# Second attention: turned rows, remote part, combination and local gate one round later, weight sum ahead of the last block transpose

## What is computed

```python
local = _local_window_attn(Q, K, V)
...
lp = jax.nn.softmax(lsc, axis=-1)
rem = jnp.einsum('bhsn,bhnd->bhsd', lp, GV)
rem = rem.transpose(0, 2, 1, 3).reshape(Bx, Sx, LATENT_DIM) @ r_out_w
...
gl = jax.nn.sigmoid(jnp.einsum('bhsd,hd->bhs', Q, gate_local_w))[..., None]
gr = jax.nn.sigmoid(jnp.einsum('bhsd,hd->bhs', Q, gate_remote_w))[..., None]
out = gl * local + gr * rem
out = out.transpose(0, 2, 1, 3).reshape(Bx, Sx, D_MODEL)
return out @ w_out
```

## Time and profile before

| | |
|---|---|
| median of 3 runs | 1703.9 us (1700.4 to 1706.74) |
| the profiled execution | 1714.27 us, its span 1712.6 us |
| busy: PE, DVE, ACT, POOL | 1511.4, 1137.9, 989.6, 931.1 us |
| mean granted clock of PE | 0.936 |

### The profile page before, as it was taken

One profiled execution on the slowest core, in us unless ns is written; L12 is line 12 of the kernel. 1 busy time (PEld: TensorE's weight loads), 2 busy tenths in 40 slices (PEclk: granted clock), 3 DMA queues, 4 the chain that ended last, 5 costly groups with the idle time before them and its releaser, 6 DMA issues.

```text
span 1712.6 us, 44507 instructions
## 1 busy us (share of the span) xinstructions
PE 1511.4 (88%) x13886; PEld 1087.7 (64%) x13887; DVE 1137.9 (66%) x2702; ACT 989.6 (58%) x2495; POOL 931.1 (54%) x1633
## 2 busy tenths in 40 slices
PE   7989999999999999998999688888888888885884
PEld 5645455555555555555999577777777777774774
DVE  5666555555555555552555498898898998995662
ACT  5544455555555555553334588888888888872442
POOL 5334555555555555554543466666666666631665
PEclk6989899999999999998999699999999999995776
DMA  9131132222211212223332122211211212215442
GB/s 278 34 83 42 51 82 57 57 57 57 55 49 52 55 50 54 55 57 73 67 68 62 30 48 45 45 41 43 46 43 41 45 43 42 44 38 113 86 93 35
DMA packets 240853, 103.39 MB, mean 60 GB/s; under 512 B 145497, under 2 KB 229274, under 8 KB 240794
## 3 DMA queue, kind: packets, MB, share of 16 engines
q1 hardware_dynamic: 230554, 89.04, 22.4%
q0 software_dynamic: 10240, 13.64, 3.8%
HBM read 57.73 MB, written 35.96 MB: 55 GB/s over the span
## 4 chain that ended last, share of the span: by engine, by line
PE 46%; ACT 16%; DVE 10%; DMA 10%; issue 7%; POOL 5%; SPq 5%; POOLq 0%; DVEq 0%; ACTq 0%
PE bankA L1887 5%; PE bankB L1933 5%; DMA remainders<-yT 4%; PE bankT L1916 4%; PE bankT L2067 4%; SPq L369 3%; DMA dq<-remainders 3%; DVE mneg L1000 3%; ACT qx L1692 3%; ACT km L1701 2%; ACT gqx L1692 2%; PE bankS L1901 2%; PE bankB L1937 2%; PE bankT L1919 2%; PE bankB L2130 2%
## 5 line engine op out<-in xcount | busy, mean ns | idle before, releaser
L682 POOL TENSOR_SCALAR_AFFINE_SELECT probs<-probs 128x512 f32<-128x512 f32 x256 | 184.0, 743 | 154.1 <-ACT probs L1578 154.1
L1578 ACT ACTIVATE probs<-bankT 128x1024 f32<-128x1024 f32 x128 | 131.1, 1024 | 190.6 <-PE bankT L1919 190.6
L999 DVE TENSOR_REDUCE mneg<-bankS 128x2 f32<-128x256 f32 x256 | 106.6, 417 | 160.2 <-PE bankS L1906 159.4
L1000 DVE TENSOR_REDUCE mneg<-bankS 128x2 f32<-128x512 f32 x256 | 174.3, 681 | 0.0
L675 POOL CAST qb<-qT 128x256 bf16<-128x256 f32 x256 | 97.5, 400 | 92.4 <-ACT qT L1573 91.7
L1916 PE MATMUL bankT<-qT,kT 37*128 37x512 f32 x512 | 138.0, 617 | 9.5 <-ACT probs L1580 6.2
L1573 ACT ACTIVATE qT<-bankA,bd 128x256 f32<-128x256 f32 x256 | 107.6, 473 | 65.5 <-PE bankA L1887 65.5
L1887 PE MATMUL bankA<-xnT,wd 128*128 128x256 f32 x480 | 144.4, 414 | 0.0
L1933 PE MATMUL bankB<-probs,vaug 128*64 128x512 f32 x512 | 142.9, 637 | 1.0 <-ACT yT L1585 1.0
L1585 ACT COPY yT<-bankB 128x512 f32<-128x512 f32 x128 | 75.1, 587 | 116.7 <-PE bankB L1937 116.7
L1367 DVE STREAM_TRANSPOSE pt<-pe 128x768 f32<-128x768 f32 x128 | 124.4, 972 | 25.9 <-ACT pe L1678 25.9
(11 more groups left out here) (320 smaller groups left out, 4286.8 us busy)
## 6 DMA issues: line engine op xcount, KB each, us to landing
rzb<-reciprocals SPq DMA_DIRECT2D x128, 128.0 KB
yT<-yT SPq DMA_DIRECT2D x64, 128.0 KB
xtab<-tab SPq DMA_DIRECT2D x32, 192.0 KB, 2.0
xs_sorted<-zeros SPq DMA_DIRECT2D x1, 4608.0 KB, 19.0
qT<-xs_sorted SPq DMA_DIRECT2D x144, 32.0 KB, 1.8
ys_sorted<-qT SPq DMA_DIRECT2D x36, 128.0 KB, 1.9
value_rows<-vrow SPq DMA_DIRECT2D x32, 128.0 KB, 1.8
vx<-value_rows SPq DMA_DIRECT2D x256, 16.0 KB, 1.8
```

The source lines that it names most:

```text
L682: pool.affine_select(out=blocks, in_=blocks, compare_op=ALU.is_ge, fill=0.0, base=0, pattern=[[0, 4], [1, P]], channel_multiplier=-1).then ...
L1000: dve.tensor_reduce(mneg[:, n.half, :, j, 1], bankS[:, :, 128:384], AX.X, ALU.max, negate=True).then_inc(S["red_done"], 1)
L1578: act.activation(pT[:, g % 2].rearrange("p e j t -> p e (j t)"), bankT[:, 0:2, :], ACT.Exp, scale=SCALE0).then_inc(S["exp_done"], 1)
```

## The change

POOL: `local_gate` of the batch before (`p`, a new argument) moves from the end of the round to behind `stream1` and `copy1`. DVE: `turn_rows` moves to the place of `combine`, `combine` goes behind the third group's `shift`, `finish` behind the second `turn`, and `weight_sum` ahead of the fourth `turn`. PE: `remote` takes the place of `project`, and `project` goes behind the value product, ahead of the gate product. What is left over for the last batch is issued behind the loops. No instruction of work is added or taken away. Later lines of the changed kernel have numbers one or two higher.

```diff
-            def step1(b, n, m, k):
+            def step1(b, p, n, m, k):
                 if m:
                     stream1(m)
                     copy1(m, True)
+                if p:
+                    local_gate(p)
                 if n:
                     weigh(n)
...
                 if m:
                     pool_latents(m)
-                if b:
-                    local_gate(b)
                 if k:
                     gather(k)
...
             with pool.Fori(1, LOOP - 1) as i:
-                step1(Batch(i, 0), Batch(i, 1), Batch(i + 1, 0), Batch(i + 1, 1))
-                step1(Batch(i, 1), Batch(i + 1, 0), Batch(i + 1, 1), Batch(i + 2, 0))
...
+                step1(Batch(i, 0), Batch(i, 0).before(), Batch(i, 1), Batch(i + 1, 0), Batch(i + 1, 1))
+                step1(Batch(i, 1), Batch(i, 0), Batch(i + 1, 0), Batch(i + 1, 1), Batch(i + 2, 0))
...
+            local_gate(Batch(LOOP, 1))
...
                 if b:
                     shift(b, 1)
                 if p:
-                    combine(p)
+                    turn_rows(p)
                 if b:
                     turn(b, 0)
                     shift(b, 2)
                 if p:
-                    finish(p)
+                    combine(p)
                 if b:
                     turn(b, 1)
+                if p:
+                    finish(p)
                 if n:
                     route(n)
...
                 if m:
                     mean1(m, True)
+                if n:
+                    weight_sum(n)
                 if b:
                     turn(b, 3)
-                if n:
-                    weight_sum(n)
-                if b:
                     shared_gated(b)
                     shared_hidden(b)
                     invert1(b)
                 if n:
                     shift(n, 0)
-                if b:
-                    turn_rows(b)
...
+            turn_rows(Batch(LOOP, 1))
             combine(Batch(LOOP, 1))
             finish(Batch(LOOP, 1))
...
                 if n:
                     latents(n, b is not None)
                 if p:
-                    project(p)
+                    remote(p)
                 if b:
                     scores(b, 3)
                 if n:
                     values(n)
+                if p:
+                    project(p)
                 if b:
                     gate(b)
                     attend(b, 0, n is None)
...
                     xt1(m, b is not None)
-                if b:
-                    remote(b)
...
+            remote(Batch(LOOP, 1))
             project(Batch(LOOP, 1))
```

## The result

The changed kernel takes 1848.7 us (median of 4 runs, 1844.9 to 1853.4) against 1702.8 for the kernel before, measured beside it: a ratio of 1.0856, 95% interval 1.0822 to 1.0889. The forecast was 1871, its range 1812 to 1930. The profiled execution took 1848.92 us, its span 1846.0, at a mean granted clock of 0.900. Lines of DVE, ACT and PE have numbers one higher than before; POOL's line 868 has kept its number.

A forecast was written before the change was run, and what follows sets the result against it. The second attention was taken as bound by a loop of waits. 29 x (4.29 stall + 1.5 clock) - 1.2 = 167 us on the profiled 1714.3 gave 1881, less 10.4 for the median: 1871 us, range 1812 to 1930.

The forecast's parts named there:

- The bound: Second attention stage, 985 to 1546 us: a loop of waits of 18.07 us a round, no engine filling it.
- The stall: DVE waits before aT for POOL's gate product, now behind the gather: 4.29 us more a round, in 29 rounds.
- The fallen clock: PE, idle 4.5 us a round, drops to half clock for 5 us once work returns: 1.5 us per round.
- the room that hides it: PE's attention products end 6.13 us after aT, DVE's last transpose 7.41; of these 1.28 us, 1.0 taken as hiding lateness.
- The sum of weights: On DVE, ahead of the last transpose: free during its 0.57 us wait for the last exponential, otherwise 0.30 us.
- The link taken out: Turned rows, remote part, then query product at the round's end: without it ACT's qs starts 0.42 us earlier per round.
- The rival "faster": Product done before DVE reaches aT, by 4.3 us after xp, so no stall: 31 x 0.42 = 13 us, 1691; chance 0.03.

The follow-up runs named there:

- The kernel with PE kept busy: The changed kernel with four unread 128x512 products added on PE ahead of the projection, filling its idle time: 1827.1 us, ratio 1.0732.
- three pairs: Weight sum ahead of, then behind the last transpose: product before gathered stream 1708.1, 1699.2; product at round's end 1696.6, 1688.6; product and turned rows back 1682.9, 1690.0 us.

## Why the prediction was right, and where it was off

*The bound.* Right: the stage is a loop of waits. That PE, DVE, ACT and POOL all do less per microsecond in the changed kernel says the same.

*The stall.* Right in place and count, and near in size. The product was to end 8.89 us after xp and aT at 9.31; in the round above they end at 1169.79 and 1170.31, 8.68 and 9.20 after the end of xp (1161.11). The stall was put at 4.29 us a round, 123 us in all. The kernel with PE kept busy, which has the stall without the fallen clock, is 124 us above the kernel before (117 by its turned rows). The wait itself is longer than the 4 us and more of the working, 5.0, as DVE came to aT 1164.89 - 1161.11 = 3.78 us after xp and not 4.3. That the product's place is the cause is shown from both sides: moved alone it costs 193 us, moved back alone the loss is gone.

*The fallen clock.* Right that it falls, and when; **its size is the step that failed**: 1.5 us a round was forecast, 0.75 to 0.86 measured. The half clock lasted a little longer with work at hand (from 1170.4 to past 1176, some 6 us) than the 5 us taken, and PE fell behind by about half of that, as the working had it: its third group of attention products ended at 1178.71 + 0.41 = 1179.12, 8.81 us after aT, where 6.13 was read at full clock, so 2.7 us late.

```profile
1178.71 0.41 PE L2192 MATMUL bankT<-gvx,pt 128*64 128x68 f32 x8
```

```profile
1181.85 0.26 ACT L1768 COPY rows<-bankT 32x128 f32<-32x128 f32 x1
```

What was mis-sized is the room that hides it, put at 1.0. From aT to the last transpose took 7.65 us (working: 7.41), and from there to the last rows 1182.11 - 1177.96 = 4.15 (3.34): 1.05 came out in this round and some 1.6 were hidden. The sum had found 1.28 and used 1.0 of it. It also missed that in the kernel before PE's third group already ended 0.37 us behind DVE's last transpose (1162.81 against 1162.44), so that this much lateness stands in the 3.34 already; with it the room is 1.65. The forecast's 1.5 less the measured 0.75, 29 times, is 22 us: what 1871 was too high by.

The Trainium skill (TensorE: Matmul & The Clock Gate, section on the clock gate) would have kept the clock within one per cent of the span. The runs show 21.6 us, 1.2% of 1848.7, give or take some 9: near that advice, and not the 44 of the forecast.

*The sum of weights.* Put at nothing while DVE waits, 0.30 where it doesn't. In the changed kernel it cost nothing, as the late PE covered it (the last two groups of products are 0.71 us apart at the median with the sum in either place). Where the stall was taken away, two of three pairs show 0.22 to 0.23 us a round; in the third PE came later than the transpose.

*The link taken out* (0.42 us a round, 13 us) is real: the version that turns the rows and multiplies the gate in the old places has 0.45 of it, and the wait ahead of qs is gone. The combination, the projection and the finishing sum moved with the remote part there, and their share was not tried apart. The rival "faster" had named POOL's queue between gather and product as its place, and asked that the product be done 4.3 us after xp. With the product ahead of the gathered stream it ended 1165.18 - 1160.97 = 4.21 after xp, and yet 1708. That condition was set too late, since DVE came to aT 3.8 us after xp and still waited 0.53, and the prediction didn't see that DVE's routing would meet POOL's stream.

## What to carry to other kernels

Work that is put off by a round takes a place in some queue, and it is the entries ahead of it there that decide: find the slowest thing they wait for (here a gather of 5.3 us that starts only when the round does) before counting what is won. When a chain is shortened on one engine, leave its partners on the other engines where their inputs come ready: with the same link cut and the turned rows and the gate's product left in place, the change won 20 us instead of losing 146. And when a long wait opens on one engine, look for a second bill on the engine behind it, here PE's clock, but count only the part by which it then comes later than the engines that it works with.

## What the runs showed of the hardware

DVE and POOL held each other up. A DVE instruction of two inputs took 0.30 us by itself and up to 0.81 when it began just after POOL's sum of two tiles (0.72 us), and ended some 0.15 us after it. The Trainium skill (SBUF — State Buffer, section "Who interferes with whom") has this as a rule: a DVE instruction with two SBUF inputs and a POOL instruction that reads SBUF contend for a shared port pair, which is an exclusive lock, and the order of issue decides which of them blocks. The rows agree in the main where DVE is second: shl and mb each paid, and shl, begun 0.27 us ahead of POOL's sum, paid nothing; but they end 0.15 us after POOL's instruction and not the 0.30 of a whole one, so not all of theirs was held up. Where POOL is second they agree less: in the round followed before, its sum began 0.04 us after mb and took 0.83 us, 0.11 more than the 0.72, where a full block would have added the 0.25 that mb still had to go.

```profile
1157.34 0.29 DVE L1342 TENSOR_TENSOR mb<-lg,lgr 128x128 bf16<-128x128 f32 x1
```

```profile
1157.38 0.83 POOL L809 TENSOR_TENSOR xa_all<-xa_all,yg 128x256 f32 x1 [0.29 <-POOL yg L804]
```

The clock: with PE idle from 1165.9 it was full until 1169 and at 0.50 by 1170, and it stayed there with PE busy 5.63 of the next 6.00 us. The idle time of 1.89 us in the kernel before had left it at 1.00.
